# A mixture of experts computed for the chosen experts only, in blocks of 128 rows from two waves of tokens

## The chip, the cores and the metric

The kernel runs on one NeuronCore of a Trainium2 chip. The metric is the device time of one execution in microseconds; three executions of the kernel before took 1513.09, 1513.53 and 1516.65 us (median 1513.53). TensorE is written PE, VectorE DVE, ScalarE ACT, GpSimd POOL, and SyncE, which here only issues DMAs, SP.

## The reference

A block of three residual layers on x of 16 x 64 tokens of 512 values, all in f32:

```python
x = x + xattn(layernorm(x), ctx)        # 16 heads of 64 over pairs of tokens, 512 context tokens
x = x + ssm(layernorm(x))               # projections, conv of 4 taps, selective scan of 16 states, out projection
x = x + moe(layernorm(x))               # below
# moe: T = 1024 tokens, E = 16 experts of I = 256, TOP_K = 4
scores = sigmoid(x @ gate_weight.T); choice = scores + e_bias
# 2 of 4 groups of experts by the sum of the two best, then the 4 best experts in them
topk_weight = scores[topk_idx] / sum
y[t] = sum over e of combine[t, e] * (silu(x @ gate_proj[e].T) * (x @ up_proj[e].T)) @ down_proj[e].T
```

The combine weight of an expert that a token did not choose is 0, so the result is the same whether that expert is computed or not.

## The kernel before, in words

The 1024 tokens are four groups g of 256 (two tiles of 128). Each group goes through attention (8 units of 32 queries x 8 heads, each with its context loaded by SP), projections, and the scan. The scan of group g runs on DVE while PE and ACT do the attention of group g + 1: 16 states, each of four DVE instructions (`scan_step`, L1074, L1077, L1080, L1084) with the decay computed by ACT (L855). The order of every engine is written out by hand in the program of that engine; engines meet at counting semaphores.

After the fourth group's projections comes the expert stage. It computes all 16 experts for all tokens as 64 jobs of one expert and 256 tokens: 48 jobs for groups 0 to 2, expert by expert, then 16 jobs for group 3, whose scan is spread over the first of them (`scan_parts`). A job is `gate_up` (48 matmuls of L634: weights and inputs are split in a rounded and a remainder part, `split_hi` on ACT and `split_lo` on DVE, and three products are summed), tanh on ACT (L902), `hidden` on DVE (L1167, L1168), `down` (four matmuls of 512 columns, L665, each shown as two records) and `add_expert` (L1179), which adds the result times the combine weight to the residual tiles kept in SBUF. Gate, up and down weights of an expert, 512 KB each, are loaded by SP once for groups 0 to 2 and once more for group 3 (`load_raw` L363, `load_down` L376); each of five raw slots is loaded again when DVE has split it. `route` (L1124) computes the combine weights of a group on DVE after its first job. `last_out_proj` (L674) is the out projection of group 3 between jobs. POOL does nothing.

Of the kernel before, what the change touches and what calls it, by code (L numbers as in the profile page):

```python
# [23 lines left out]
F32R = mybir.dt.float32r  # L24
# [32 lines left out]
PIECES = 2  # L57
RAW = 5
CA = G - 1
JA = E * CA  # L60
JOBS = JA + E
SCAN_FROM = 4
SCAN_JOBS = 39
OUT_JOB = SCAN_FROM + SCAN_JOBS + 1
BK_PER_NORM = 512 // (NT * P)
# [19 lines left out]
def job(j):  # L85

    return (j // CA, j // CA, j % CA) if j < JA else (E + j - JA, j - JA, G - 1)


def first_job(c):  # L90
    return c if c < CA else JA


def x_item(j):

    return j + 2 * min(j + 1, CA) + (2 if j >= JA else 0)


def y_item(j):

    return j + (1 if j >= OUT_JOB else 0)


def last_job(k):

    return CA * (k + 1) - 1 if k < E else JA + k - E


def splits(j):


    out = []
    for k in range(1, 2 * E):
        f = CA * k if k < E else JA + k - E
        at = (max(f - 4, -1), f - 3) if k <= E else (f - 2, f - 2)
        out += [(k, p) for p in range(PIECES) if at[p] == j]
    return out


# [4 lines left out]
def scan_parts(j):  # L124

    return [(q // SCAN_PARTS, q % SCAN_PARTS) for q in range(SCAN_PARTS, NS * SCAN_PARTS)
            if SCAN_FROM + (q - SCAN_PARTS) * SCAN_JOBS // ((NS - 1) * SCAN_PARTS) == j]


def perceiver_block(nc, x, ctx_t, ctx_n, wq_t, wk, wv_t, xp_t, dt_t, bc_t, ow_t, gate_t,  # L130
                    eg_t, eu_t, ed_t, params, bc_dram, out):
    with ExitStack() as es:
# [7 lines left out]
        xs_ = sb("x_tokens", G * NT * D)  # L140
# [3 lines left out]
        sb8 = nrm_[0:H, 0:NU * Q].rearrange("p (u h i) -> p u h i", u=NU, h=H)  # L144
        bcT = nrm_[0:2 * NS, 0:GT]
        comb_ = sb("comb", G * NT * E)
        xT_ = sb("normed_t", DC * GT)
        xT = xT_[:, :].rearrange("p (c t) -> p c t", c=DC)
# [6 lines left out]
        acc = acc_[:, :].rearrange("p (k t) -> p k t", k=NBK)  # L155
# [3 lines left out]
        bcs = [bcs_[:, s * 2 * GT:(s + 1) * 2 * GT].rearrange("p (w t) -> p w t", w=2) for s in range(2)]  # L159
# [3 lines left out]
        ident = par[:, C_ID:C_ID + P]  # L163

        lgs = [sb(f"route_logits_{c}", NT * E)[:, :] for c in range(G)]
        sc, sfc, gs = (sb(f"route_{n}", NT * E)[:, :] for n in ("score", "choice", "group"))
        st_ = sb("stats", 6 * G * NT)
        mv_ = sb("mean_var", 2 * NT)
        rstd = sb("rstd", NT)
# [1165 lines left out]
```

## Time and profile before

| what | value |
|---|---|
| median of three runs | 1513.53 us |
| the profiled execution (its span; the page shows no time around it) | 1514.9 us |
| PE busy | 1281.5 us, 85% |
| DVE busy | 1157.1 us, 76% |
| ACT busy | 599.0 us, 40% |
| DMA moved | 128.47 MB, mean 85 GB/s |
| attention, projections, scans of groups 0 to 2 | up to about 858 us |
| expert stage | about 858 us to the end |

A page of the profile gives busy time by engine, the span in 40 slices, the DMA queues, the chain of work that ended last, and groups of instructions. A wait is named by what ended it. Matmuls are pipelined, so the busy time of a PE group overlaps itself; lengths of runs of matmuls in the chain are the better measure. PEclk is TensorE's granted clock as a share of 2.4 GHz; 0.50 is 1.2 GHz.

### The profile page before, as it was taken

What the parts mean: (1) busy time and instruction counts of PE and PEld (TensorE: products, weight loads), DVE (VectorE), ACT (ScalarE), POOL (GpSimd) and SP (SyncE); (2) the same over time, 40 slices, a digit from 0 to 9 for tenths busy, and PEclk for the clock granted to TensorE, in tenths of its full rate; (3) what the DMA queues carried; (4) which work ended last, traced back from release to release, by engine and by line L of the source; (5) the groups of instructions that cost most, each with busy time, mean ns of one, the idle gap of its engine ahead of it and who ended that gap; (6) DMA issues with size and microseconds to landing.
All of it is one profiled execution on the core that took longest, in us unless ns stands there. A gap on an engine that the chain in (4) does not pass through costs nothing.

```text
span 1514.9 us, 16115 instructions
## 1 busy us (share of the span) xinstructions
PE 1281.5 (85%) x6400; PEld 965.9 (64%) x6400; DVE 1157.1 (76%) x1001; ACT 599.0 (40%) x1229; POOL 0.2 (0%) x4
## 2 busy tenths in 40 slices
PE   6998578868859758858758898999999999998998
PEld 4776446646536547536537586777777777676775
DVE  1201899998999998999998848979888888446554
ACT  4432754554655535745536611131313131022220
POOL 0000000000000000000000000000000000000000
PEclk9999878988978978979879789999999999999999
DMA  7333013324013324013314201222222312114553
GB/s 247 101 121 127 6 25 116 104 63 133 8 49 91 118 54 128 10 49 110 89 57 145 91 22 35 86 61 70 56 77 63 84 49 63 56 44 152 168 160 103
DMA packets 95930, 128.47 MB, mean 85 GB/s; under 512 B 4976, under 2 KB 70640, under 8 KB 95856
## 3 DMA queue, kind: packets, MB, share of 16 engines
q1 hardware_dynamic: 95856, 127.45, 27.9%
q8 instruction: 51, 0.84, 0.2%
q14 instruction: 23, 0.19, 0.0%
HBM read 125.21 MB, written 2.23 MB: 84 GB/s over the span
## 4 chain that ended last, share of the span: by engine, by line
DVE 55%; PE 31%; ACT 8%; issue 3%; DMA 2%; DVEq 0%; ACTq 0%; SPq 0%
DVE state L1077 16%; PE bank L634 11%; DVE y_acc L1084 8%; DVE state L1074 8%; DVE state L1080 7%; PE bank L591 6%; PE bank L665 6%; ACT decay L855 4%; DVE x_tokens L1179 3%; DVE w_lo L1161 2%; DMA queries_ctx<-in_dt_t 2%; PE bank L520 2%; PE bank L545 2%; DVE hidden L1168 2%; DVE hidden L1167 2%
## 5 line engine op out<-in xcount | busy, mean ns | idle before, releaser
L1077 DVE TENSOR_TENSOR_SCAN state<-decay,state 128x2048 f32<-128x2048 f32 x64 | 282.9, 4420 | 8.3 <-ACT decay L855 7.2
L665 PE MATMUL bank<-w_down,hidden 128*128 128x512 f32 x512 | 232.1, 596 | 5.2 <-DVE x_tokens L1179 5.2
L634 PE MATMUL bank<-x_hi,w_hi 128*128 128x256 f32 x1024 | 192.6, 312 | 12.2 <-DVE hidden L1168 7.5
L855 ACT ACTIVATE decay<-delta_odd,params 128x256 f32<-128x256 f32 x256 | 106.3, 498 | 197.7 <-DVE state L1077 186.8
L634 PEld LDWEIGHTS bank<-x_hi,w_hi 128*128 128x128 f32 x1024 | 150.3, 198 | 43.5 <-issue 30.4
L520 PE MATMUL bank<-ctx,queries_ctx 128*128 128x256 f32 x512 | 151.8, 449 | 22.2 <-ACT queries_ctx L748 22.2
L634 PE MATMUL bank<-x_hi,w_lo 128*128 128x256 f32 x1024 | 168.9, 288 | 0.0
L634 PE MATMUL bank<-x_lo,w_hi 128*128 128x256 f32 x1024 | 168.7, 288 | 0.0
L902 ACT ACTIVATE hidden<-bank 128x512 f32<-128x512 f32 x64 | 38.0, 594 | 327.6 <-PE bank L665 321.5
L665 PEld LDWEIGHTS bank<-w_down,hidden 128*128 128x128 f32 x512 | 93.3, 191 | 100.5 <-issue 94.2
L1084 DVE TENSOR_TENSOR y_acc<-y_acc,state 128x2048 f32<-128x2048 f32 x64 | 146.7, 2292 | 2.3
L1080 DVE TENSOR_TENSOR state<-state,bc_bcast 128x2048 f32<-128x2048 f32 x64 | 146.2, 2284 | 1.4
L1167 DVE SCALAR_TENSOR_TENSOR hidden<-hidden,bank 128x512 f32<-128x512 f32 x64 | 43.8, 685 | 135.0 <-ACT hidden L902 134.8
L634 PEld LDWEIGHTS bank<-x_hi,w_lo 128*128 128x128 f32 x1024 | 145.6, 198 | 0.0
L634 PEld LDWEIGHTS bank<-x_lo,w_hi 128*128 128x128 f32 x1024 | 145.6, 197 | 0.0
L545 PE MATMUL bank<-probs,ctx 128*128 128x256 f32 x512 | 132.7, 417 | 14.9 <-ACT probs L782 14.9
L520 PEld LDWEIGHTS bank<-ctx,queries_ctx 128*128 128x128 f32 x512 | 109.1, 224 | 53.5 <-ACT queries_ctx L748 23.8
L855 ACT ACTIVATE decay<-delta_even,params 128x256 f32<-128x256 f32 x256 | 107.0, 500 | 79.7 <-DVE state L1077 71.3
L545 PEld LDWEIGHTS bank<-probs,ctx 128*128 128x128 f32 x512 | 104.4, 209 | 40.6 <-ACT probs L782 17.1
L591 PE MATMUL bank<-normed_t,queries_ctx 128*128 128x256 f32 x512 | 112.3, 381 | 2.4 <-DMA queries_ctx<-in_dt_t 1.3
L591 PEld LDWEIGHTS bank<-normed_t,queries_ctx 128*128 128x128 f32 x512 | 96.8, 190 | 19.5 <-DMA queries_ctx<-in_dt_t 3.7
L1161 DVE TENSOR_TENSOR w_lo<-raw_w,w_hi 128x1024 fp32r<-128x1024 f32 x64 | 77.0, 1224 | 33.3 <-ACT w_hi L883 31.9
(128 smaller groups left out, 1328.1 us busy)
## 6 DMA issues: line engine op xcount, KB each, us to landing
ctx<-in_ctx_t SPq DMA_DIRECT2D x32, 512.0 KB, 6.3
ctx<-in_ctx_n SPq DMA_DIRECT2D x32, 512.0 KB, 3.5
bc_bcast<-bc_scratch SPq DMA_DIRECT2D x64, 256.0 KB, 5.1
raw_w<-in_eg_t SPq DMA_DIRECT2D x32, 512.0 KB, 4.3
raw_w<-in_eu_t SPq DMA_DIRECT2D x32, 512.0 KB, 4.0
w_down<-in_ed_t SPq DMA_DIRECT2D x32, 512.0 KB, 4.8
queries_ctx<-in_dt_t SPq DMA_DIRECT2D x4, 2048.0 KB, 10.0
queries_ctx<-in_xp_t SPq DMA_DIRECT2D x4, 2048.0 KB, 14.8
```

Of the source, the lines that this page charges most:

```text
L520: pe.matmul(o, QT[:, k, c, qb * P:(qb + 1) * P], ctxT[n % 2][:, c, :], start=(c == 0), stop=False)
L545: mm = pe.matmul(b[:, cc * Q:(cc + 1) * Q], ctxN[n % 2][:, j, c * P:(c + 1) * P], probT[n % 2][:, j, :], start=(j == 0), stop=(j == KC - 1))
L591: mm = pe.matmul(b[:, kk * GT:(kk + 1) * GT], w[:, c, (k + kk) * P:(k + kk + 1) * P], xT[:, c, :], start=(c == 0), stop=(c == DC - 1))
L634: mm = pe.matmul(o, w[a](k), x[b](k), start=(q == 0), stop=(q == len(terms) - 1))
L665: mm = pe.matmul(b[t][:, :], hid[j % 2][:, i * GT + t * P:i * GT + (t + 1) * P], w_dn[k % 2][:, i, :], start=(i == 0), stop=(i == IC - 1))
L855: ins = act.activation(dA[n % 2][:, k * GT:(k + 1) * GT], dlt[g % 2][:, k, :], ACT.Exp, scale=par[:, c:c + 1])
L1074: step(dve.tensor_tensor(h3, u[g % 2], bs, ALU.mult))
L1077: dve.tensor_tensor_scan(h, dA[n % 2], h, 0.0, ALU.mult, ALU.add).then_inc(scan_rd, 1)
L1080: step(dve.tensor_tensor(h3, h3, cs, ALU.mult))
L1084: dve.tensor_tensor(acc_[:, :], acc_[:, :], h, ALU.add).then_inc(step_done, 1)
L1161: dve.tensor_tensor(lo, raw[q % RAW], hi, ALU.subtract).then_inc(w_rdy, 1)
L1167: step(dve.scalar_tensor_tensor(out=o, in0=o, scalar=1.0, in1=b[0][:, :], op0=ALU.add, op1=ALU.mult))
```

## The change

The expert stage is replaced. Groups 0 and 1 are wave 0, groups 2 and 3 wave 1, of 512 tokens each. For a group, `ffn_norm` (DVE) writes the normed rows, `ffn_logits` (PE, ACT) transposes them and computes logits, `route` (DVE) ranks and masks as before, `positions` (PE, matmuls with 16 columns) counts for each token and expert the earlier tokens of the wave that chose it, and `slots` (DVE) makes from that, for each of a token's four experts, a row of a DRAM tensor: expert e has 512 rows of its own. `dispatch` on POOL scatters each tile's rows there by eight indirect DMAs a group. `block_table` (DVE) turns the counts of a wave into a table in SBUF of 31 entries (expert, first row): as many blocks of 128 rows as 512 x 4 choices can need with 16 experts. All 31 blocks are run, whatever the counts; those beyond the last used one read rows that hold zeros or leftovers and nothing reads their results.

For a block q, SP reads the two entries into registers, loads gate, up and down weights of that expert (three DMAs of 512 KB, 4 KB for each partition, to one of NW = 3 slots) and the 128 rows (256 KB, one of NX = 3 slots), and stores the block's result (256 KB) to DRAM. PE transposes the rows (4), does gate and up as 4 plain f32 matmuls of 512 columns, transposes the hidden values (2) and does down as 2 matmuls of 512 columns. ACT copies the transposes and results out of PSUM. After a wave, `collect` on POOL gathers four rows of each token by indirect DMAs, `combine` (DVE) adds them with their weights, and the tile is stored. The split products, `split_hi`, `split_lo` and `add_expert` are gone.

The norms, logits, routes and slots of groups 0 and 1 are done during the attention of groups 2 and 3; those of group 2 and the scan of group 3 during wave 0; those of group 3, with the out projection of its scan, between the waves. The collecting and combining of wave 0 runs beside wave 1. During the first 14 attention units POOL writes zeros over the scatter tensors: 40 DMAs of up to 512 rows, 41.4 MB in all. The core of the diff:

```diff
--- before.py
+++ after.py
+WAVES = ((0, 1), (2, 3))
+WAVE_OF = [w for g in range(NGR) for w in range(len(WAVES)) if g in WAVES[w]]
+WTILES = [[TILE0[g] + t for g in gs for t in range(NTS[g])] for gs in WAVES]
+CAP = [P * len(t) for t in WTILES]
+BLOCKS = [(TOPK * c + E * (P - 1)) // P for c in CAP]
+BLOCK0 = [sum(BLOCKS[:w]) for w in range(len(WAVES))]
+ROWS = [E * c + b * P - TOPK * c for c, b in zip(CAP, BLOCKS)]
...
+CLEARS = [(w, r, min(r + CLEAR_ROWS, ROWS[w])) for w in range(len(WAVES)) for r in range(0, ROWS[w], CLEAR_ROWS)]
+CLEAR_UNITS = range(1, 15)
...
+NW = 3
+NX = 3
...
+            def load_block_w(w, j):
+                q = BLOCK0[w] + j
+                sp.wait_ge(tab_rdy, w + 1)
+                e = sp.value_load(tabs[w][j:j + 1, 0:1], min_val=0, max_val=E - 1)
+                if q >= NW:
+                    sp.wait_ge(y_full, q - NW + 1)
+                for p, t in enumerate((eg_t, eu_t)):
+                    sp.dma_start(wb_[q % NW][:, p * DC * I:(p + 1) * DC * I],
+                                 t[bass.DynSlice(e, 1)].rearrange("o (p c) i -> p (o c i)", p=P)).then_inc(gu_in[q % NW], 16)
+                sp.dma_start(wb_[q % NW][:, 2 * DC * I:],
+                             ed_t[bass.DynSlice(e, 1)].rearrange("o (p c) d -> p (o c d)", p=P)).then_inc(dn_in[q % NW], 16)
...
+            def load_block_x(w, j):
+                q = BLOCK0[w] + j
+                if j == 0:
+                    sp.wait_ge(tab_rdy, w + 1)
+                    sp.wait_ge(dispatched, 16 * TOPK * sum(len(WTILES[v]) for v in range(w + 1)))
+                row = sp.value_load(tabs[w][j:j + 1, 1:2], min_val=0, max_val=ROWS[w] - P)
+                if q >= NX:
+                    sp.wait_ge(xt_full, q - NX + 1)
+                sp.dma_start(xb[q % NX], xd[w][bass.DynSlice(row, P)]).then_inc(xb_in[q % NX], 16)
+            def store_block_y(w, j):
+                q = BLOCK0[w] + j
+                sp.wait_ge(y_rdy, q + 1)
+                sp.dma_start(yd[w][j * P:(j + 1) * P], yb[q % NX]).then_inc(yb_out[q % NX], 16)
+            def store_out(n, t):
...
+                for j in range(BLOCKS[w]):
+                    if j + NX < BLOCKS[w]:
+                        load_block_x(w, j + NX)
+                    if j + NW < BLOCKS[w]:
+                        load_block_w(w, j + NW)
+                    store_block_y(w, j)
...
-            def split_matmul(o, w, x, chunks):
-                terms = [(a, b, k) for a, b in ((0, 0), (0, 1), (1, 0)) for k in range(chunks)]
-                for q, (a, b, k) in enumerate(terms):
-                    mm = pe.matmul(o, w[a](k), x[b](k), start=(q == 0), stop=(q == len(terms) - 1))
-                return mm
...
-            def gate_up(j):
-                k, e, c = job(j)
-                b = x_pair(x_item(j))
-                if first_job(c) == j:
-                    pe.wait_ge(xm_rdy, c + 1)
-                x_parts = [(lambda q, v=v: v[:, q * GT:(q + 1) * GT]) for v in xm[c % CA]]
-                for p in range(PIECES):
-                    pe.wait_ge(w_rdy, k * PIECES + p + 1)
-                    for i in range(IC):
-                        w_parts = [(lambda q, v=v: v[p][:, q, i * P:(i + 1) * P]) for v in w_gu[k % 2]]
-                        mm = split_matmul(b[p][:, i * GT:(i + 1) * GT], w_parts, x_parts, DC)
-                mm.then_inc(x_full, 1)
...
-            def down(j):
-                k, e, c = job(j)
-                b = y_pair(y_item(j))
-                if j == 0:
-                    pe.wait_ge(d_free, jd.n)
-                    pe.wait_ge(a_free, ja.n)
-                pe.wait_ge(down_in[k % 2], 16 * (k // 2 + 1))
-                pe.wait_ge(h_rdy, j + 1)
-                for t in range(NT):
-                    for i in range(IC):
-                        mm = pe.matmul(b[t][:, :], hid[j % 2][:, i * GT + t * P:i * GT + (t + 1) * P],
-                                       w_dn[k % 2][:, i, :], start=(i == 0), stop=(i == IC - 1))
+            def block_x_t(q):
...
+            def block_x_t(q):
+                pe.wait_ge(xb_in[q % NX], 16 * (q // NX + 1))
+                if q >= 2:
+                    pe.wait_ge(xt_rdy, q - 1)
+                v = xb[q % NX].rearrange("t (p c) -> t c p", c=DC)
+                for c in range(DC):
+                    mm = pe.transpose(bank[q % 2][:, c * P:(c + 1) * P], v[:, c, :], ident)
+                mm.then_inc(xt_full, 1)
+            def gate_up(q):
+                pe.wait_ge(xt_rdy, q + 1)
+                pe.wait_ge(gu_in[q % NW], 32 * (q // NW + 1))
+                if q >= 2:
+                    pe.wait_ge(h_rdy, q - 1)
+                o = bank[2 + q % 2][:, :].rearrange("p (g i) -> p g i", g=2)
+                for c in range(DC):
+                    mm = pe.matmul(o, xbT[q % 2][:, c, :], w_gu[q % NW][:, :, c, :], start=(c == 0), stop=(c == DC - 1))
+                mm.then_inc(gu_full, 1)
+            def hidden_t(q):
+                pe.wait_ge(h_rdy, q + 1)
+                b = job_a()
+                v = hid[q % 2].rearrange("t (p c) -> t c p", c=IC)
+                for c in range(IC):
+                    mm = pe.transpose(b[:, c * P:(c + 1) * P], v[:, c, :], ident)
+                mm.then_inc(a_full, 1)
+                ha[q] = ja.n
+            def down(q):
+                pe.wait_ge(a_free, ha.pop(q))
+                pe.wait_ge(dn_in[q % NW], 16 * (q // NW + 1))
+                if q >= 2:
+                    pe.wait_ge(y_rdy, q - 1)
+                for c in range(IC):
+                    mm = pe.matmul(bank[4 + q % 2][:, :], hidT[q % 2][:, c, :], w_dn[q % NW][:, c, :],
+                                   start=(c == 0), stop=(c == IC - 1))
                 mm.then_inc(y_full, 1)
-            def last_out_proj():
-                b = y_pair(y_item(OUT_JOB) - 1)
-                pe.wait_ge(step_done, NS * G)
...
+            def experts(w):
+                q0, n = BLOCK0[w], BLOCKS[w]
+                pe.wait_ge(d_free, jd.n)
+                for j in range(-2, n + 1):
+                    if j + 2 < n:
+                        block_x_t(q0 + j + 2)
+                    if 0 <= j + 1 < n:
+                        gate_up(q0 + j + 1)
+                    if 0 <= j - 1:
+                        down(q0 + j - 1)
+                    if 0 <= j < n:
+                        hidden_t(q0 + j)
+                    if w == 0 and j == 0:
+                        ffn_logits(NGR - 2)
+                    if w == 0 and j == 4:
+                        positions(NGR - 2)
             pe.wait_ge(par_in, 16)
             pe.wait_ge(ones_rdy, 1)
-            norm_transposes(0, NT)
+            norm_transposes(0, NTS[0])
             attention(0)
...
+            experts(0)
+            pe.wait_ge(y_rdy, BLOCK0[1])
+            out_proj(NGR - 1)
+            ffn_logits(NGR - 1)
+            positions(NGR - 1)
+            experts(1)
...
+            def keep_y(q):
+                act.wait_ge(y_full, q + 1)
+                if q >= NX:
+                    act.wait_ge(yb_out[q % NX], 16 * (q // NX))
+                act.activation(yb[q % NX], bank[4 + q % 2][:, :], ACT.Copy).then_inc(y_rdy, 1)
...
-            def split_lo(k, p):
-                q = k * PIECES + p
-                dve.wait_ge(w_hi_rdy, q + 1)
-                hi, lo = (v[p].rearrange("p c i -> p (c i)") for v in w_gu[k % 2])
-                dve.tensor_tensor(lo, raw[q % RAW], hi, ALU.subtract).then_inc(w_rdy, 1)
...
+            def hidden(q):
+                b = bank[2 + q % 2]
+                dve.wait_ge(th_rdy, q + 1)
+                o = hid[q % 2]
+                step(dve.scalar_tensor_tensor(out=o, in0=o, scalar=1.0, in1=b[:, 0:I], op0=ALU.add, op1=ALU.mult))
+                dve.tensor_tensor(o, o, b[:, I:2 * I], ALU.mult).then_inc(h_rdy, 1)
...
+                if w == 0:
+                    add_tiles(NGR - 1)
+                    ffn_norm(NGR - 1)
+                    route(NGR - 1)
+                    slots(NGR - 1)
+                    block_table(1)
+                    out_slots(1)
+            for i, t in enumerate(WTILES[1]):
+                combine(len(WTILES[0]) + i, t)
...
+                pool.wait_ge(s_full, n)
+                v = xd[w][first:end].rearrange("(p r) d -> p r d", p=P)
+                pool.dma_start(v, fx_[:, 0:D].unsqueeze(1).to_broadcast([P, (end - first) // P, D])).then_inc(cleared, 16)
...
+            def dispatch(c):
+                pool.wait_ge(slot_rdy, c + 1)
+                for t in range(NTS[c]):
+                    for k in range(TOPK):
+                        i = (TILE0[c] + t) * TOPK + k
+                        pool.indirect_dma_start(xd[WAVE_OF[c]], bass.IndirectOffsetOnAxis(slot[:, i:i + 1].bitcast(U32), 0),
+                                                fx[:, t, :], None).then_inc(dispatched, 16)
...
+                    pool.indirect_dma_start(yg_[n % 2][:, k, :], None, yd[w],
+                                            bass.IndirectOffsetOnAxis(yslot[:, i:i + 1].bitcast(U32), 0))\
+                        .then_inc(yg_in[n % 2], 16)
...
```

## Rows read from the trace of the kernel before

**Rows 1.** The page of the profile: the span, and busy time of each engine.
```profile
span 1514.9 us, 16115 instructions
...
PE 1281.5 (85%) x6400; PEld 965.9 (64%) x6400; DVE 1157.1 (76%) x1001; ACT 599.0 (40%) x1229; POOL 0.2 (0%) x4
```

**Rows 2.** Windows (length, busy by engine, PEclk, DMA share, GB/s): attention, experts.
```profile
617.00:779.00 162.00, 120.17 (x496) 85.00 (x496) 158.59 (x73) 89.69 (x222) 0.00 (x0) 0.86 0.24 63
858.00:1514.90 656.90, 623.72 (x3632) 488.56 (x3632) 464.37 (x534) 152.52 (x258) 0.00 (x0) 0.97 0.28 83
```

**Rows 3.** Chain that ended last: start us, us, what.
```profile
1251.12 5.75 PE bank L634 x48
1256.87 3.44 PE bank L665 x8
...
1311.98 13.73 PE bank L674 x32
```

**Rows 4.** Groups of instructions by line and form: busy us, mean ns, idle before.
```profile
L1077 DVE TENSOR_TENSOR_SCAN state<-decay,state 128x2048 f32<-128x2048 f32 x64 | 282.9, 4420 | 8.3 <-ACT decay L855 7.2
L665 PE MATMUL bank<-w_down,hidden 128*128 128x512 f32 x512 | 232.1, 596 | 5.2 <-DVE x_tokens L1179 5.2
...
L1084 DVE TENSOR_TENSOR y_acc<-y_acc,state 128x2048 f32<-128x2048 f32 x64 | 146.7, 2292 | 2.3
...
L1161 DVE TENSOR_TENSOR w_lo<-raw_w,w_hi 128x1024 fp32r<-128x1024 f32 x64 | 77.0, 1224 | 33.3 <-ACT w_hi L883 31.9
...
L902 ACT ACTIVATE hidden<-bank 128x512 f32<-128x512 f32 x64 | 38.0, 594 | 327.6 <-PE bank L665 321.5 <-PE bank L634 6.1
...
L1095 DVE TENSOR_TENSOR rank_scratch<-route_choice 128x256 f32<-128x256 f32 x8 | 3.4, 421 | 0.1
```

**Rows 5.** Timeline of PE (start us, us): eight 128x128 transposes.
```profile
826.17 1.04 PE L620 MATMUL bank<-params,normed 128*128 128x128 f32 x8
```

**Rows 6.** Timeline of SP's queue, 787 to 790 us: start us, issue us.
```profile
788.24 0.37 SPq L348 DMA_DIRECT2D queries_ctx<-in_dt_t  x1
788.66 0.51 SPq L349 DMA_DIRECT2D queries_ctx<-in_xp_t  x1
```

**Rows 7.** Windows: large loads in flight, the clock around idle PE.
```profile
788.00:792.00 4.00, 0.37 (x2) 0.37 (x3) 3.35 (x9) 0.30 (x1) 0.00 (x0) 0.50 0.48 81
791.60:797.70 6.10, 5.00 (x16) 2.81 (x16) 5.55 (x9) 1.27 (x3) 0.00 (x0) 0.50 0.96 388
797.70:802.00 4.30, 4.00 (x19) 3.25 (x18) 4.27 (x2) 0.37 (x1) 0.00 (x0) 1.00 1.03 408
856.70:859.20 2.50, 0.01 (x1) 0.00 (x0) 2.43 (x4) 2.47 (x6) 0.00 (x0) 0.98 0.23 73
863.50:872.80 9.30, 9.21 (x43) 9.24 (x44) 5.40 (x11) 3.96 (x5) 0.00 (x0) 0.50 0.61 187
381.30:384.70 3.40, 1.17 (x9) 0.84 (x8) 2.29 (x6) 3.38 (x5) 0.00 (x0) 0.99 0.01 2
384.70:388.10 3.40, 3.40 (x8) 1.85 (x7) 3.33 (x7) 1.92 (x2) 0.00 (x0) 0.51 0.00 0
```

**Rows 8.** DMA issues of the page: KB each, median us from issue to landing.
```profile
ctx<-in_ctx_n SPq DMA_DIRECT2D x32, 512.0 KB, 3.5
...
raw_w<-in_eg_t SPq DMA_DIRECT2D x32, 512.0 KB, 4.3
```

**Rows 9.** Timeline of DVE: first and last of 33 instructions of one route.
```profile
895.21 0.18 DVE L1128 TENSOR_SCALAR route_score<-route_logits 128x32 f32<-128x32 f32 x1
...
903.57 0.19 DVE L1155 TENSOR_TENSOR comb<-route_score,route_group 128x32 f32<-128x32 f32 x1
```

**Rows 10.** Timelines, 787 to 832 us: norm of one group on DVE, an ACT table load.
```profile
788.30 1.42 DVE L989 BATCH_NORM_STATS2 stats<-x_tokens 128x6 f32<-128x512 f32 x2
...
790.57 1.00 DVE L1001 TENSOR_SCALAR normed<-x_tokens,mean_var,rstd 128x512 f32<-128x512 f32 x2
...
830.91 1.28 ACT L724 ACT_TABLE_LOAD   x1
```

More of the change, by code:

```diff
@@ new lines, in attention_units @@
+                    if k == 1 and g >= 2:
+                        positions(g - 2)
+                    if now:
+                        scan_decay(g - 1, now[0], NBK // 2)
+                    copy_probs(n)
+                    for s in now[1:]:
+                        scan_decay(g - 1, s)
+                keep_ctx(g, NUS[g] - 1)
+            def projections(g):
+                late = list(range(NS - TAIL + 1, NS)) if g > 0 else []
+                norm_std(NTS[g])
+                norm_copy(xT[g], NTS[g])
@@ L995, in norm_stats, with norm_apply @@
                 step(dve.reciprocal(std[:, first:first + n], std[:, first:first + n]))
-            def norm_apply(tile0, slot, var=mv_, std=rstd, first=0):
-                for t in range(NT):
+            def norm_apply(tile0, n, slot, var=mv_, std=rstd, first=0):
+                for t in range(n):
                     q = first + t
@@ L1120, in free_logits @@
[L1120 to L1133 removed]
+                step(dve.tensor_reduce(out, rk1.rearrange("p (r j) -> p r j", j=n), AX_X, ALU.add))
@@ new lines, in hidden, with combine @@
+            def hidden(q):
[4 more added lines that the diff above has]
+                dve.tensor_tensor(o, o, b[:, I:2 * I], ALU.mult).then_inc(h_rdy, 1)
+            def combine(n, t):
+                dve.wait_ge(yg_in[n % 2], 16 * TOPK * (n // 2 + 1))
+                tile = xs[:, t, :]
+                for k in range(TOPK):
+                    c = t * TOPK + k
+                    ins = dve.scalar_tensor_tensor(out=tile, in0=yg_[n % 2][:, k, :], scalar=wk[:, c:c + 1], in1=tile,
+                                                   op0=ALU.mult, op1=ALU.add)
+                    if k < TOPK - 1:
+                        step(ins)
+                ins.then_inc(comb_done, 1)
@@ L1219, in _ @@
             scan_inputs(0)
-            scan_step(0, 0, parts=(0, 1, 2))
-            scan_step(0, 0, parts=(3,))
-            for g in range(G - 1):
+            dve.wait_ge(cst_rdy, 1)
+            step(dve.tensor_copy(iota[:, :], iota_i[:, :]))
+            scan_step(0, 0)
+            for g in range(NGR - 1):
                 for s in range(LEAD):
@@ L1285, in _ @@
-            add_expert(JOBS - 1)
-            dve.nop().then_inc(out_rdy, 1)
+            for w in range(len(WAVES)):
+                q0, n = BLOCK0[w], BLOCKS[w]
+                for j in range(-1, n):
+                    if j + 1 < n:
+                        hidden(q0 + j + 1)
+                    if w == 0:
+                        if j == 1:
+                            route(NGR - 2)
+                        if j == 5:
+                            slots(NGR - 2)
+                        for state, part in scan_parts(j):
+                            scan_step(NGR - 1, state, parts=(part,))
+                    elif j >= 2 and j % 2 == 0 and (j - 2) // 2 in range(len(WTILES[0])):
+                        combine((j - 2) // 2, WTILES[0][(j - 2) // 2])
+                if w == 0:
+                    add_tiles(NGR - 1)
[4 more added lines that the diff above has]
+                    out_slots(1)
```

1015 lines of the change are left out of this document (554 added, 461 removed).

## The prediction

> **What bounds the kernel now.** The page comes first [rows 1]: PE is busy for 85% of 1514.9 us and DVE for 76%, neither bound everywhere, so the span has to be cut into stages. The windows [rows 2] do that. While a group's attention runs beside the scan of the group before, DVE is busy for 158.6 of 162 us: whatever is added to DVE there lengthens the span by itself. From 858 us on it is PE, 623.7 of 656.9 us at a clock of 0.97. The chain of waits [rows 3] gives the step of that stage: 48 matmuls of gate and up in 5.75 us, four of down in 3.44 us, so 9.19 us a job and 588 us for 64 jobs; 13.7 us of out projection and the norms and logits make up the rest. Down's 3.44 us for four also gives the price of a plain f32 matmul of 512 columns at full clock, 0.86 us.
>
> **PE's work after.** A block has four transposes (eight take 1.04 us [rows 5], so 0.52), four matmuls for gate and up (3.44), two transposes (0.26) and two for down (1.72): 5.9 us. Two waves of 31 blocks make 184 us each, 368 against 588. DVE has, in wave 0, 15 scan states of 4.42 + 3 x 2.29 = 11.3 us [rows 4], 31 times two instructions of 256 columns at 0.42 (26 us), a route of 8.5 us (33 instructions from 895.21 to 903.76 [rows 9]) and about 3 us of slots: 208 us, 6.7 a block. Were these the bounds, the change would win. They aren't, by the order in which the loads are released.
>
> **The new wait: a block's loads hang on the block before.** The weights of block j+3 go into the slot of block j and are issued when down of j has ended (y_full). PE's order is rows of j+4, gate and up of j+3, down of j+1: between down of j and gate and up of j+3 stand only six transposes, 0.8 us. Down of j+1, which releases the next load, comes behind that gate and up. So from one y_full to the next PE first waits for a load, then works 0.52 + 3.44 + 1.72 = 5.7 us, and nothing of this overlaps. The rows are worse placed than the weights. On SP's queue each turn is: rows of j+3, weights of j+3 (held for y_full of j), store of block j. The rows of j+4 are therefore issued behind the weights of j+3 and the store, and they are what PE transposes ahead of gate and up of j+3.
>
> **L, from y_full to the landing of those rows.** Issues take 0.37 to 0.51 us each [rows 6]: three for weights, one store, one for rows, about 2.4 us, and between the last two a read of a register from the table, which no row shows. Its ends are 0 and the 3.5 us of a small load's round trip [rows 8]; I take 1, near the low end, as a few bytes need no large transfer. The rows are then issued at 3.4 us. They share the DMA engines with the rest: the first large load at 788.24 meets a window to 792 with a DMA share of 0.48, that is 1.92 us busy, so data flow 1.84 us after an issue, and then at 388 to 408 GB/s with the engines 96 to 103% busy [rows 7]. A turn moves 3 x 524 KB + 2 x 262 KB = 2.10 MB, 5.1 us at 408. With 0.3 us to complete, L = 1.84 + 5.1 + 0.3 = 7.3 us. Ends: gate and up alone (1.05 MB) 4.4 us, and 9.4 us where the register read costs 3.5 and the rows then land in 3.5. The Trainium skill (DMA: Bandwidth & Descriptors, Specifications) gives a core's HBM limit as about 358 GB/s; the windows show 408, so the measurement decides, and by the page L would be 7.7 and the total some 20 us more.
>
> **The clock.** PE idles about 7 us in each turn. In the trace the clock is at 0.50 from 2.5 us after PE stopped at 856.7, and stays there for 9.3 us after it resumed at 863.5; after the idle before 791.6 for 6.1; after the short idle before 384.7 for 3.4 [rows 7]. I take 4.75, between the shorter two, since matmuls here are dense: they do 2.4 of the 5.7 us of work, the other 3.3 run at full clock, 8.1 in all. Turn: 7.3 + 8.1 = 15.4, say 15.5 us. Ends: 4.4 + 5.7 = 10.1 (never cold, early landing) and 9.4 + 11.4 = 20.8 (all cold).
>
> **The sum**, against the profiled span, which is 1.4 us (0.1%) over the median of the runs.
> - Attention, DVE-bound: two routes 17, two times slots 6, a block table and output slots 5 (some 20 instructions of 0.2 to 0.4 us), three norms of 3.3 us (788.30 to 791.57) and an ACT table load of 1.28 with its wait [rows 10], 15. Out: a norm 3.3, two w_lo of 1.2, four instructions of 512 columns at 0.6 [rows 4], 8. Net 35.
> - The 41.4 MB of zeros run on POOL's queue beside context loads. Some 23 MB fall in the eight units of group 0, whose PE is not covered by a scan; at 408 GB/s they take 56 us, and a context load may be late by a few: 5, between 0 and 56. The rest hides behind DVE. First rows of wave 0, issue and landing: 5. Logits of group 2 inside wave 0: 5. PE thus has 858 + 35 + 5 + 5 + 5 = 908 before the waves count.
> - Waves: 3 blocks each are loaded ahead, 7 us each; 28 at 15.5: 455 each, 910.
> - Between the waves nothing overlaps: copy 0.6, out projection 13.7, add 0.7, norm and table load 4.6, transposes and copies 2.2, logits 3, table load and exp 1.5, route 8.5, positions and copy 3.4, slots 3, eight scatters and their landing 15.5, first rows 4, PE cold at times 1.3: 62.
> - After the last block: copy and store 4.1, sixteen gathers in four tiles with only two buffers, combine 2.5 a tile, store 3.5: 36. No row shows an indirect DMA. Its ends are an ordinary issue, 0.37, and one that lands before the next, 4.3 [rows 6, 8]; I take 1.5, nearer to the issue, because only issue has to be serial. The ends move both terms together by -27 and +62.
>
> 908 + 910 + 62 + 36 = 1916; I say **1915 us**.
>
> **Rivals.** *Early landing or a warm clock (1690 us, 0.17).* If the weights' landing alone counts, or the clock holds, the turn is 10 to 13 us; at 11.5 the sum is 56 x 4 = 224 less. For it: the queue may let the small rows through. Against: the engines are 96% busy while large loads are in flight [rows 7].
> *Colder and later (2165 us, 0.15).* The register read and the address taken from a register cost several us and every block is cold: turn 20, 56 x 4.5 = 252 more. For it: PE idles 7 us in each turn, and 9.3 us cold have been seen; nothing of before reads a register.
> *The loads are hidden and the change wins (1412 us, 0.04).* The mechanism is the prefetch: if L is over before PE arrives, wave 0 goes at DVE's 7.0 and wave 1 at PE's 6.1: 908 + 217 + 189 + 62 + 36. Break-even with 1515 needs a turn of (1515 - 908 - 62 - 36 - 42) / 56 = 8.3 us, that is L of 2.6 us or less at a full clock. A single load of 512 KB takes 3.5 to 4.3 [rows 8], and three of them, a store and the rows are asked for here.
> *The change doesn't do what it says (0.01).* Were unused blocks skipped, fewer turns would run; but the loops over 31 have no branch.
>
> **Numbers.** The forecast has 0.63. Its own range: a turn of 12.6 (4.4 + 8.1) takes 162 off and quick POOL issues 27, about 1725; cold for 9.3 us (work 4.65 in it, 1.05 after: 10.4, turn 17.7) adds 123 and slow POOL issues 35, about 2075. From 1720 to 2080 it also takes in a part of the first two rivals, 8 in 10. A measurement of this kernel tells 0.3% (about 4.5 us) from no change. Faster only with the hidden loads or skipped blocks: 0.05; within 0.3%: 0.01; slower: 0.94.
>
> **What would show it.** Weight loads waiting for down on SP; PE's rows transposes waiting for the DMA of the rows, about 7 us in each of 56 turns; y_full every 15.5 us in both waves alike, though only wave 0 has the scan; a granted clock near 0.65 in the waves; DMA near 135 GB/s (2.10 MB a turn); DVE done early in wave 0; PE without blocks for some 60 us between the waves. Wrong would be: y_full every 6 to 8 us, a wave 0 clearly longer than wave 1 (then DVE's scan sets it), or a wait for the weights but none for the rows.

## The result, and the profile after the change

The changed kernel takes 2033.14 us (median of 4 runs, 2026.34 to 2036.74), the kernel before beside it 1513.97 (1513.09 to 1516.65): a ratio of 1.342, interval 1.338 to 1.345. The forecast was slower, 1915 us, range 1720 to 2080. The direction, the mechanism and the range held; 118 us are missing from the sum.

The page of the profile after: span, busy time, the chain's shares, and DMA issues (KB each, us from issue to landing). The first lines answer to [rows 1], the last ones to [rows 8].

```profile
span 2035.0 us, 12399 instructions
...
PE 1193.0 (59%) x3988; PEld 747.9 (37%) x3988; DVE 990.2 (49%) x934; ACT 617.9 (30%) x1350; POOL 119.5 (6%) x113
...
PE 35%; DVE 27%; DMA 22%; SPq 6%; issue 5%; ACT 4%; POOL 0%; POOLq 0%; DVEq 0%; ACTq 0%
DMA block_x<-dispatched 16%; PE bank L723 15%; DVE state L1218 8%; PE bank L742 5%; PE bank L691 5%; DVE y_acc L1225 4%; DVE state L1221 4%; DVE state L1215 4%; DMA ctx<-in_ctx_t 4%; PE bank L713 3%; PE bank L618 2%; SPq L409 2%; DMA queries_ctx<-in_dt_t 2%; PE bank L641 2%; SPq L420 1%
...
ctx<-in_ctx_t SPq DMA_DIRECT2D x32, 512.0 KB, 7.6
...
block_x<-dispatched SPq DMA_DIRECT2D x62, 256.0 KB, 6.1
```

PE has 88 us less to do than before and DVE 167 less, and yet the span is 520 us longer. In the expert stage no engine is busy throughout any more; DVE's 27% of the chain is the attention and scans of before. What has come in is a line of the chain that did not exist, the landing of a block's rows, with 16% of the chain.

The windows by stage (columns as in [rows 2]: length, busy time and instructions by engine, PEclk, DMA share, GB/s): wave 0, what lies between the waves, wave 1, and what follows the last block.

```profile
926.00:1439.00 513.00, 249.06 (x573) 124.79 (x571) 199.64 (x166) 102.52 (x237) 12.73 (x8) 0.70 0.39 127
1439.00:1507.00 68.00, 23.92 (x78) 15.36 (x78) 20.98 (x79) 5.24 (x9) 15.32 (x16) 0.66 0.38 146
1507.00:2002.00 495.00, 250.18 (x558) 123.31 (x558) 37.78 (x78) 56.84 (x123) 7.56 (x8) 0.71 0.37 126
2002.00:2035.00 33.00, 0.15 (x1) 0.00 (x0) 12.03 (x16) 0.60 (x1) 16.01 (x16) 0.57 0.55 167
```

The two waves are nearly equally long, though DVE has 200 us of work in the one and 38 in the other: DVE does not set them. PE is busy for half of each at a clock of 0.70, DMA for 0.38. So neither engine nor bandwidth fills the stage: it goes by a chain in which each waits for the other.

One turn of wave 1 in the timeline, PE first (start us, us, idle before and releaser), then SP's queue:

```profile
1708.48 1.88 PE L742 MATMUL bank<-expert_w,hidden_t 128*128 128x512 f32 x4
1710.20 0.39 PE L732 MATMUL bank<-params,hidden 128*128 128x128 f32 x2
1719.00 1.13 PE L713 MATMUL bank<-params,block_x 128*128 128x128 f32 x4 [8.41 <-DMA block_x<-dispatched]
1719.92 5.27 PE L723 MATMUL bank<-expert_w,block_x_t 128*128 128x512 f32 x8
1725.03 1.88 PE L742 MATMUL bank<-expert_w,hidden_t 128*128 128x512 f32 x4
```

```profile
1710.54 0.35 SPq L409 DMA_DIRECT2D expert_w<-in_eg_t  x1
...
1711.89 0.42 SPq L428 DMA_DIRECT2D expert_out<-block_y  x1
1713.07 0.34 SPq L423 DMA_DIRECT2D block_x<-dispatched  x1
```

Down of one block ends at 1710.36 (1708.48 + 1.88) and releases, 0.18 us later, five issues (up and down at 1710.98 and 1711.45, not shown), the rows last. They land at 1719.00, 8.64 us behind down, and only then PE works: 7.9 us to the end of the next down. Over a wave a turn is 17.3 us in wave 0 and 17.0 in wave 1 (27 turns each, 950.2 to 1418.3 and 1521.8 to 1980.8). The waits of the whole kernel (us in total, times, longest), and PE's last wait of wave 0:

```profile
PE bank L713 <- DMA block_x<-dispatched: 497.9, 56, 11.9
...
SPq L409 <- PE bank L742: 728.9, 56, 26.2
```

```profile
1425.70 5.67 PE L723 MATMUL bank<-expert_w,block_x_t 128*128 128x512 f32 x8 [5.26 <-issue]
```

SP's queue waits for down 56 times, 28 in each of two waves, as counted. The equal count of PE's waits for rows is a coincidence: two of the 56 (11.91 and 0.23 us) come ahead of wave 0's first blocks. In the turns there are 27 such waits a wave, 54 in all with 485.8 us, since the rows of blocks 4 to 30 are the late ones. The 28th turn of each wave has no rows left to wait for and stands only for the last block's gate and up weights: it takes 12.9 and 13.6 us. The wait for rows is thus 9.0 us on average, and with the 0.23 us in which PE still transposes hidden, L is 9.2 us.

### The profile page after: what moved, and what is told of

It reads as the page before. It is cut to its first block, busy times and chain, and to the rows that moved or that the text cites. A ratio compares the mean times of both kernels' runs of the same rounds, so it can differ in the third digit from the quotient of the medians.

```text
span 2035.0 us, 12399 instructions
## 1 busy us (share of the span) xinstructions
PE 1193.0 (59%) x3988; PEld 747.9 (37%) x3988; DVE 990.2 (49%) x934; ACT 617.9 (30%) x1350; POOL 119.5 (6%) x113
## 4 chain that ended last, share of the span: by engine, by line
PE 35%; DVE 27%; DMA 22%; SPq 6%; issue 5%; ACT 4%; POOL 0%; POOLq 0%; DVEq 0%; ACTq 0%
DMA block_x<-dispatched 16%; PE bank L723 15%; DVE state L1218 8%; PE bank L742 5%; PE bank L691 5%; DVE y_acc L1225 4%; DVE state L1221 4%; DVE state L1215 4%; DMA ctx<-in_ctx_t 4%; PE bank L713 3%; PE bank L618 2%; SPq L409 2%; DMA queries_ctx<-in_dt_t 2%; PE bank L641 2%; SPq L420 1%
## 5 line engine op out<-in xcount | busy, mean ns | idle before, releaser
L1362 DVE SCALAR_TENSOR_TENSOR hidden<-hidden,bank 128x256 f32<-128x256 f32 x62 | 26.1, 421 | 785.3 <-ACT hidden L1027 785.3
L713 PE MATMUL bank<-params,block_x 128*128 128x128 f32 x248 | 68.1, 428 | 526.6 <-DMA block_x<-dispatched 497.9
L723 PE MATMUL bank<-expert_w,block_x_t 128*128 128x512 f32 x496 | 324.0, 813 | 11.2 <-issue 11.2
L1218 DVE TENSOR_TENSOR_SCAN state<-decay,state 128x2048 f32<-128x2048 f32 x64 | 282.9, 4420 | 14.4 <-ACT decay L973 13.6
L713 PEld LDWEIGHTS bank<-params,block_x 128*128 128x128 f32 x248 | 45.1, 218 | 539.0 <-DMA block_x<-dispatched 496.5
L723 PEld LDWEIGHTS bank<-expert_w,block_x_t 128*128 128x128 f32 x496 | 132.0, 281 | 164.7 <-issue 164.3
L1023 ACT ACTIVATE block_x_t<-bank 128x512 f32<-128x512 f32 x62 | 37.0, 596 | 447.2 <-PE bank L713 447.1
L641 PE MATMUL bank<-probs,ctx 128*128 128x256 f32 x512 | 131.0, 413 | 17.8 <-ACT probs L897 13.8
L1501 POOL DMA_INDIRECT dispatched<-ffn_x,slot x32 | 58.0, 1812 | 1118.7 <-DVE slot L1307 1110.2
L641 PEld LDWEIGHTS bank<-probs,ctx 128*128 128x128 f32 x512 | 103.2, 207 | 43.3 <-ACT probs L897 15.9
L742 PE MATMUL bank<-expert_w,hidden_t 128*128 128x512 f32 x248 | 117.0, 594 | 2.9 <-ACT hidden_t L1037 2.9
L1027 ACT ACTIVATE hidden<-bank 128x256 f32<-128x256 f32 x62 | 23.8, 383 | 277.9 <-PE bank L723 277.9
L1215 DVE TENSOR_TENSOR state<-u_even,bc_bcast 128x2048 f32<-128x2048 f32 x32 | 73.4, 2292 | 4.1 <-DMA bc_bcast<-bc_scratch 2.7
L1215 DVE TENSOR_TENSOR state<-u_odd,bc_bcast 128x2048 f32<-128x2048 f32 x32 | 73.3, 2291 | 1.0
```

The costliest lines, as they stand in the source:

```text
L641: mm = pe.matmul(b[:, cc * Q:(cc + 1) * Q], ctxN[n % 2][:, j, c * P:(c + 1) * P], probT[n % 2][:, j, :], start=(j == 0), stop=(j == KC - 1))
L713: mm = pe.transpose(bank[q % 2][:, c * P:(c + 1) * P], v[:, c, :], ident)
L723: mm = pe.matmul(o, xbT[q % 2][:, c, :], w_gu[q % NW][:, :, c, :], start=(c == 0), stop=(c == DC - 1))
L742: mm = pe.matmul(bank[4 + q % 2][:, :], hidT[q % 2][:, c, :], w_dn[q % NW][:, c, :], start=(c == 0), stop=(c == IC - 1))
L1215: step(dve.tensor_tensor(h3, u[g], bs, ALU.mult))
L1218: dve.tensor_tensor_scan(h, dA[n % 2][:, 0:sw], h, 0.0, ALU.mult, ALU.add).then_inc(scan_rd, 1)
```

## The experiments

All are variants of the changed kernel; the kernel before ran beside each (1514.99 us beside the first four, 1516.19 and 1515.78 beside the others). In their order below they are called rows4, w4, rows4_w4, tiny_w, warm8, late_zeros, rows6_w4_zeros and rows6_w4_spread. rows4, w4 and tiny_w ran once each, warm8 twice, the others four or five times. Diffs are cut to their core.

### A fourth slot for rows

```diff
+NR = 4
...
-        xb = [sb(f"block_x_{s}", D)[:, :] for s in range(NX)]
+        xb = [sb(f"block_x_{s}", D)[:, :] for s in range(NR)]
...
-                    if j + NX < BLOCKS[w]:
-                        load_block_x(w, j + NX)
+                    if j + NR < BLOCKS[w]:
+                        load_block_x(w, j + NR)
```

NX stays 3 for the results, block_y.

> Four slots for a block's rows in place of three, so that rows of block j+4 are issued ahead of the weights of block j+3 and a whole turn before PE wants them. Theory A (each turn waits for loads that are released by the down of two blocks before, and the rows land last, 8.5 us after it): the rows leave the path, gate and up weights stay on it with some 5.5 us, and the transposes run inside that wait. Turn 17.1 - 3.0 - 0.9 = 13.2, clock permitting, so about 2035 - 56 x 3.9 = 1817 us. Rival B (the DMA engines or SP cannot deliver 2.1 MB and its issues faster, whatever the order): turn unchanged, about 2035.

Measured: 1843.35 us, 190 less than the changed kernel and 26 more than expected. The timeline of PE in one turn with ACT's copy of the transposed rows, and PE's largest wait:

```profile
1706.19 1.88 PE L743 MATMUL bank<-expert_w,hidden_t 128*128 128x512 f32 x4
...
1708.13 0.65 PE L714 MATMUL bank<-params,block_x 128*128 128x128 f32 x4
...
1708.86 0.60 ACT L1024 ACTIVATE block_x_t<-bank 128x512 f32<-128x512 f32 x1
...
1713.72 6.27 PE L724 MATMUL bank<-expert_w,block_x_t 128*128 128x512 f32 x8 [4.95 <-issue]
```

```profile
PE bank L724 <- issue: 271.1, 55, 5.4
```

The rows are there already (their transposes follow down at once) and PE stands at gate and up instead, 5.65 us behind down (1708.07 to 1713.72). The trace names no releaser for it; by the program gate and up wait for the copied rows (there at 1709.46), for the hidden values of two blocks before (long done) and for their weights, whose first issue was at 1708.24, behind that down. So it is the weights. A turn is 13.6 us in both waves, 3.5 less. The terms: PE stands for 5.65 us behind down where it stood for 9.2 (the rows' extra lateness, 3.5), the transposes now run inside the wait (0.9), and gate and up takes 6.27 us instead of 5.27, which gives 1.0 back and was not in the expectation. Behind the wait for rows stands the second wait that the prediction names, the weights' own.

### A fourth slot for weights

```diff
-NW = 3
+NW = 4
+NPRE = 3
...
             sp.wait_ge(ys_rdy, NGR)
+            for j in range(NPRE, NW):
+                load_block_w(0, j)
```

Ahead of wave 0 three blocks' weights are loaded in the attention, as before, and the fourth behind it.

> Four slots for weights, three for rows, so weights come one turn earlier but the rows are still issued behind weights and store of the block before. Theory A: nothing is gained, as the rows are what lands last: 2035 +- 15 us. A rival by which the weights set the turn: turn falls to 8 or less, total near 1530 us.

Measured: 2022.92 us in its one run, 10 under the median of the changed kernel and 3 under its fastest. The wait for the rows stands where it was, and wave 1 still takes 17.0 us a turn:

```profile
PE bank L716 <- DMA block_x<-dispatched: 500.9, 55, 16.1
```

The weights are now a block ahead, and wave 1's turns gain nothing from it, since SP's queue is in order: the rows are issued behind the weights and the store that wait for down, whatever slot the weights go to.

### Both

The two diffs together.

> Four slots for both. Theory A: no load hangs on the block before any more; wave 0 goes at DVE's 6.8 us a block, wave 1 at PE's 6.0 to 6.4, so the waves take about 420 instead of 1015 us: about 1450 us, ratio to before 0.96. Rival B (bandwidth or issue binds): turn 12 or more, at least 1780 us. With part of the engines' time lost to contention, turns of 8 give about 1520.

Measured: 1568.43 us, ratio 1.034 (1.030 to 1.038): 465 us less than the changed kernel, but 118 more than expected. Two turns of PE in wave 1:

```profile
1303.24 1.88 PE L746 MATMUL bank<-expert_w,hidden_t 128*128 128x512 f32 x4
...
1305.67 3.60 PE L727 MATMUL bank<-expert_w,block_x_t 128*128 128x512 f32 x8
1309.11 1.88 PE L746 MATMUL bank<-expert_w,hidden_t 128*128 128x512 f32 x4
...
1313.67 1.13 PE L717 MATMUL bank<-params,block_x 128*128 128x128 f32 x4 [2.46 <-DMA block_x<-dispatched]
1314.60 4.66 PE L727 MATMUL bank<-expert_w,block_x_t 128*128 128x512 f32 x8
```

One turn is 5.87 us (1303.24 to 1309.11), PE's own work as the prediction summed it (5.9). The next waits again for rows, and behind the idle time gate and up takes 4.66 instead of 3.60. 29 waits for rows make 116.6 us, 16.9 of them the one ahead of wave 0. What the expectation missed: one more slot moves the rows one turn ahead, and a turn that has shrunk to 5.9 us is shorter than their way (issued 2.5 us behind down, landing 6 later).

### Hardly any weights

A block's loads after the first three take 128 of the 1024 columns of each third; the number and order of issues stay.

```diff
+                n = DC * I if j < NW else 128
-                    sp.dma_start(wb_[q % NW][:, p * DC * I:(p + 1) * DC * I], ...)
+                    sp.dma_start(wb_[q % NW][:, p * DC * I:p * DC * I + n], ...[:, 0:n])
```

> The weights of a block after the first three are loaded only to 128 of 1024 columns of each third (512 B for a partition in place of 4 KB), so most of the weights are left out; order, waits and number of DMAs are those of the changed kernel. If the 1.57 MB ahead of the rows delay them (theory A), the rows land at about 2.6 + 3.0 = 5.6 instead of 8.5 us after down, turn about 13.9, total about 1855 us. If it is the chain of issues and the latency of a load by itself (rival C), the turn stays within 1 us of 17.1, total over 1980.

Measured: 1882.76 us. The page's issue line of the rows, and PE's wait in one turn of wave 1:

```profile
block_x<-dispatched SPq DMA_DIRECT2D x62, 256.0 KB, 2.6
```

```profile
1706.79 1.88 PE L743 MATMUL bank<-expert_w,hidden_t 128*128 128x512 f32 x4
...
1713.95 1.13 PE L714 MATMUL bank<-params,block_x 128*128 128x128 f32 x4 [5.06 <-DMA block_x<-dispatched]
```

The rows land 2.6 us after their issue instead of 6.1, so 3.5 us of their way is the weights' data ahead of them; L is 5.3 (1708.67 to 1713.95) and the turn 13.6 in wave 1, as expected. In wave 0 it is 15.3, which was not. SP's queue there:

```profile
1181.14 0.42 SPq L429 DMA_DIRECT2D expert_out<-block_y  x1
1181.62 0.42 SPq L398 DMA_DIRECT2D bc_bcast<-bc_scratch  x1
1183.23 0.35 SPq L424 DMA_DIRECT2D block_x<-dispatched  x1
```

In most second turns the scan's 256 KB broadcast of B and C stands between the store and the rows; the rows of this one reached PE at 1187.72, 7.9 us after PE stopped. The turns mostly alternate, 16.8 and 13.8. The 28 us over the expectation are these.

### TensorE kept busy in the wait

```diff
-                pe.wait_ge(xb_in[q % NX], 16 * (q // NX + 1))
                 if q >= 2:
                     pe.wait_ge(xt_rdy, q - 1)
+                for _ in range(8 if q % BLOCKS[0] >= NX else 0):
+                    pe.matmul(bank[q % 2][:, :], ident, ow[:, 0, :], start=True, stop=True)
+                pe.wait_ge(xb_in[q % NX], 16 * (q // NX + 1))
```

> Turn theory (a turn of a wave is L, the way from the last down matmul over weights and rows to the landed rows, plus the work behind it, and a cold TensorE only stretches that work): eight matmuls that nobody reads (128 columns of the identity by 512 columns of out_w) stand ahead of TensorE's wait for the rows, so that it is busy in most of the 8.5 us of L. L stays at 8.5 us. If TensorE is then granted its higher clock, gate/up falls from 5.3 to about 3.5 us and the rest by about 0.5, the turn goes from 17.1 to about 15, and over 56 turns some 110 us go: 2033 to about 1920, granted clock from 0.77 to 0.85 or more. Rival: the clock does not matter or the dummies take as long as L themselves (8 x 0.87 us cold is 7 us): 2033 within 20 us or above it.

Measured: 1958.76 us, ratio 1.291 (1.287 to 1.295) against 1.342. The timeline of one turn:

```profile
1771.21 7.03 PE L711 MATMUL bank<-out_w,params 128*128 128x512 f32 x16
1779.42 0.75 PE L715 MATMUL bank<-params,block_x 128*128 128x128 f32 x4 [1.17 <-DMA block_x<-dispatched]
1780.00 3.60 PE L725 MATMUL bank<-expert_w,block_x_t 128*128 128x512 f32 x8
1783.44 1.88 PE L744 MATMUL bank<-expert_w,hidden_t 128*128 128x512 f32 x4
```

L is 8.3 us (1771.15 to 1779.42) and the work behind it 5.9. Granted clock in wave 1: 0.99 (1545 to 1900 us), where it was 0.70. Turns of 14.2 us are the rule there, 14.8 the mean, 15.9 in wave 0. Adding work to the busiest path shortens the kernel by 74 us: that is what the higher clock gives back, less what the dummies cost. The rival's price for them was misread: eight in 7 us is the higher level, as here; at the lower one each of the two records of such a matmul takes 0.85 us (gate and up of rows4, 1714.71 to 1718.12), so eight would take some 13.6 us, an estimate, and outlast L. The gain fell short of the expected 110 by the dummies ahead of the fourth block of each wave, whose rows come without such a wait, so that they stand there for 7 us in full (the first down is at 957.4 for 950.2, and from the last down of wave 0 to the first of wave 1 it is 91.7 us for 84.8), and by wave 0's broadcasts.

### The zeros later

```diff
-CLEAR_UNITS = range(1, 15)
+CLEAR_UNITS = (8,) * 8 + (9, 10, 11, 12, 13, 14)
```

> Theory: the zeros written to memory in the units of group 0 (23 of the 40 writes, 1 MB each in three descriptors' worth of POOL issue) slow the context loads there, and that cost group 0's attention 24 us (dt_t asked for at 146.06 instead of 122.24). Moved to units 8 to 14, where VectorE sets the pace and the queues are at less than half their rate, they should cost nothing: dt_t of group 0 back at 122 to 125, the total at 2009 to 2014 (2033 less 20 to 24). Rival: the cost moves with the zeros, since the context loads there are needed as soon: 2025 or more, and dt_t of the later groups later by what the first gains.

Measured: 2027.61 us, ratio 1.336 (1.333 to 1.339) against 1.342 (1.338 to 1.345), a gain of about 6 us at the edge of what can be told. The periods between the loads of dt_t, a projection's weights asked for when a group's attention ends, show why. Before (groups 0 to 2), the changed kernel (0 to 2), and this one (0 and 1, then the stretch in which its zeros go out):

```profile
0.00:122.24 122.24, 104.39 (x504) 77.91 (x504) 18.73 (x46) 51.11 (x107) 0.20 (x4) 1.00 0.43 146
122.24:343.52 221.28, 157.25 (x648) 116.30 (x648) 188.20 (x112) 115.66 (x258) 0.00 (x0) 0.84 0.26 75
343.52:565.82 222.30, 169.12 (x680) 119.89 (x680) 212.07 (x122) 118.86 (x266) 0.00 (x0) 0.85 0.26 76
```

```profile
0.00:146.06 146.06, 113.75 (x504) 82.80 (x504) 19.77 (x48) 51.14 (x107) 17.91 (x32) 0.93 0.77 285
146.06:370.62 224.56, 154.89 (x648) 114.09 (x648) 188.44 (x115) 115.98 (x258) 12.39 (x17) 0.83 0.45 153
370.62:610.51 239.89, 171.46 (x710) 123.96 (x710) 224.47 (x176) 123.15 (x273) 22.03 (x8) 0.84 0.26 79
```

```profile
0.00:127.68 127.68, 106.60 (x504) 79.52 (x504) 19.77 (x48) 51.14 (x107) 18.16 (x32) 0.97 0.61 216
127.68:362.20 234.52, 159.76 (x648) 117.40 (x648) 188.43 (x115) 115.87 (x258) 12.43 (x17) 0.78 0.58 206
...
110.00:150.00 40.00, 26.84 (x121) 19.12 (x122) 5.12 (x13) 6.24 (x11) 4.55 (x7) 0.69 1.02 401
```

Group 0 gains 18.4 us and group 1 gives 10 back. Its DVE work is the same (188.43 us); the first scan step comes 60.2 us behind the load of dt_t (187.8), 51.6 before (197.7 behind 146.06), because dt_t and x_proj, which the scan needs, are loaded while 23 zero writes fill the queues (share 1.02). The zeros' cost moved with them, as the rival said, though not in full.

### Six slots for rows, four for weights, the zeros later

> Six row slots, four weight slots and the late zeros. Theory: with four and four a turn is TensorE's own 5.9 us except where the rows, issued 2.5 us behind a down matmul and landing 6 us later, come late: 117 us in 29 waits, and the cold matmuls behind each. With six slots the rows are asked for two turns sooner, so those waits go, and the zeros give back 22: 1568 - 22 - about 90 = 1440 to 1480, which is faster than before (ratio about 0.96). Rival: DMA is the bound by then (1.5 MB of weights and 0.5 MB of rows in 5.9 us are 357 GB/s, where 408 was the most seen): the waits turn into waits for the weights, gate/up waits instead of the transposes, and the total stays at 1530 to 1560.

Measured: 1491.45 us, ratio 0.984 (0.981 to 0.986): 1.6% below the kernel before, and 11 us above the expected band. Turns are 8.2 us in wave 0 and 6.2 in wave 1. A stretch of wave 1 in the windows, the largest of PE's waits in wave 0 (900 to 1180 us), and ACT at one of them:

```profile
1280.00:1420.00 140.00, 133.49 (x405) 68.10 (x405) 29.68 (x60) 39.67 (x91) 7.57 (x8) 1.00 1.00 360
```

```profile
PE bank L727 <- ACT block_x_t L1027: 45.0, 12, 12.2
```

```profile
1154.30 3.30 ACT L977 ACTIVATE decay<-delta_odd,params 128x256 f32<-128x256 f32 x8 [4.67 <-DVE state L1222]
1157.51 0.57 ACT L1027 ACTIVATE block_x_t<-bank 128x512 f32<-128x512 f32 x1
```

In wave 1 the waits for rows are gone; PE is busy for 95% at its higher level and the DMA engines for all of the time at 360 GB/s, so PE and DMA are both at their bound: 2.10 MB a turn at 360 are 5.8 us, PE's work is 5.9. In wave 0 the copy of the transposed rows stands in ACT's queue behind a decay that waits for the scan on DVE, 45 us in 12 waits. No run changes ACT's order, so this rests on the trace alone. It is DVE reaching PE through ACT's order, where the prediction had expected DVE's sum alone (6.7 to 7.0 us a block).

### The zeros one unit later still

```diff
-CLEAR_UNITS = (8,) * 8 + (9, 10, 11, 12, 13, 14)
+CLEAR_UNITS = range(9, 15)
```

> As rows6_w4_zeros, but the zeros start one unit of keys later (units 9 to 14 in place of 8 to 14, seven writes behind each), so that none stands in the queues when dt_t and x_proj of group 0 are loaded. Theory: in late_zeros 23 writes went out together at 97.2 us, the queues were full from 110 to 150 us (share 1.02, 401 GB/s), and of the 18.4 us that group 0's attention gained, the wait for u_even gave 8.5 back. With the new place the first scan step starts at about 178 us instead of 187.8, the total is 1478 to 1485. Rival: the zeros are in the way of the keys of group 1 instead (their writes and 208 to 342 GB/s of loads fall together between 230 and 310 us), and the total stays within 3 us of 1491 or is above it.

Measured: 1489.14 us, ratio 0.981 (0.979 to 0.983); not told apart from the version before it, so the rival held. The first scan step did start sooner, at 172.8 us (178 was expected) where it was at 185.5 in the version before it and at 187.8 with the late zeros alone. Group 0's attention, with no zero written before its end, and the stretch in which DVE is then idle for more than a quarter:

```profile
0.00:121.60 121.60, 104.24 (x504) 77.80 (x504) 19.77 (x48) 51.12 (x107) 0.84 (x9) 1.00 0.43 146
...
270.00:310.00 40.00, 26.54 (x92) 19.15 (x90) 28.47 (x16) 17.57 (x45) 1.19 (x2) 0.73 1.01 398
```

The first line is the kernel before's again, clock, DMA share and rate included: the 24 us that the changed kernel loses there are the zeros'. In the version before this one DVE was busy for 35.0 us of that second stretch. dt_t of group 1 is asked for at 356.45, of group 3 at 843.92 (rows6_w4_zeros: 361.20, 844.92). Three places for 41 MB of zeros have each cost something; leaving them out wasn't tried, because the rows that no token fills would then be read without having been written.

## Why the prediction was right, and by how much its terms were off

The sizes, from the profiled span: forecast 908 + 910 + 62 + 36 = 1916; measured 918.6 + 520.4 + 68 + 495 + 33 = 2035.

- **The new wait: right.** The turn is L plus the work behind it, on rows first and weights behind them. Taking the rows' lateness away gave 3.5 us a turn, the weights' slot alone nothing, both together brought PE's own 5.9 us in one turn of two. The 28 turns a wave, the equal waves (within 0.3 us a turn) and the DMA rate (forecast 135 GB/s, seen 126 to 127) are as foretold; the clock is 0.70, 0.65 was forecast. The count was one too high for the rows: they are waited for in 27 turns a wave, and the last one, on weights alone, is 2 to 3 us shorter than the 15.5 that the sum takes for it.
- **L: mis-sized, and this is most of the miss.** 9.2 us on average, 7.3 forecast; 1.9 in each of 54 turns are 103 us. The turn as a whole is 17.2 against the 15.5 taken, as the work behind L is 0.1 shorter and 15.4 had been rounded up: that makes 90 of the 119 us, less 4.5 in the two last turns. The other terms: 11 ahead of wave 0, some 20 at the head and tail of the waves (the wait of 7.9 for group 2's logits is one, and 5 for it stood in the 908), 6 between them, -3 at the end. The part of L that was mis-sized is the rate. The issues were nearly right: the rows went out 2.7 us behind down (3.4 forecast) and the gap that holds the register read is 0.76 us (1 taken). Data flow from about 1711.6 us, 1.1 behind the first issue, where 1.84 was taken; so the start was even a little early. But they flow more slowly. The changed kernel in the turn above, the last line being the middle of the flow:

```profile
1709.00:1712.00 3.00, 1.59 (x6) 0.68 (x4) 0.84 (x2) 0.94 (x3) 0.00 (x0) 1.00 0.12 38
1712.00:1719.00 7.00, 0.00 (x0) 0.00 (x0) 0.00 (x0) 0.00 (x0) 0.00 (x0) 0.57 0.81 283
1713.00:1718.00 5.00, 0.00 (x0) 0.00 (x0) 0.00 (x0) 0.00 (x0) 0.00 (x0) 0.50 0.88 302
```

  2.09 MB (38 x 3.0 and 283 x 7.0) took 7.4 us to the start of PE, where 5.1 and another 0.3 to complete, for which there was no row, were forecast from the 408 GB/s of a stretch full of queued loads [rows 7]. Not only the beginning and the end are thin: in the middle too the share is 0.88 and the rate 302 GB/s. Why, no run shows. Even with the engines busy throughout, wave 1 of rows6_w4_zeros shows 360. The Trainium skill (DMA: Bandwidth & Descriptors, Specifications) has about 358 GB/s as a core's limit, which the prediction set aside for the 408: 358 is within 1% of that full wave, but the 401 of late_zeros' stretch of zeros is again above it, so no run here shows it to be a limit. The prediction's own sum by that figure is off: 2.10 MB at 358 are 5.9 us, so L would be 8.0 and the total some 40 us more, where it says 7.7 and 20.
- **The work behind L: right.** 7.9 us in the turn shown against 8.1. warm8 gives its warm value, 5.9 (5.7 forecast), so the cold clock costs some 2.0 us of work a turn.
- **The zeros: mis-sized.** 5 us forecast between 0 and 56; group 0 took 23.8 longer (146.06 against 122.24), and with no zeros in it 121.6. The page has the context loads landing after 7.6 us where it had 6.3 before, PE waited for them for 11 us, and the mean clock of the period is 0.93 for 1.00. How much of the 24 reaches the end is less clear: moving the zeros gained 6 us in all, and the kernel without them wasn't run.
- **DVE's additions: about right, 35 forecast.** Group 1's period grew by 3.3 us, group 2's by 17.6, group 3's by 20.8: 41.7. Of group 2's, 12.4 are DVE work (224.47 against 212.07) and the rest waits. With the zeros it is 65.5 at the dt_t of group 3; 60.6 are left where PE takes the first rows, at 918.6 for the 858 of before (it waits 11.9 for them, 5 forecast), and 50 were forecast, 5 of them for logits that in fact stand inside wave 0 (a wait of 7.9 us there).
- **Between the waves 68 for 62, after the last block 33 for 36.** No row had shown an indirect DMA; nearly all gathers and 18 of the 32 scatters, all eight of those between the waves among them, issue in 0.95 us with 0.30 between, 1.25, where 1.5 was taken between 0.37 and 4.3. (Twenty-four of them at 4.3 would have added 67 us, where the prediction has 62.)
- **Rivals.** "Early landing" needed a turn of 10 to 13, "colder and later" one of 20; both are excluded by 17.0 to 17.3. The total itself lies nearly as close to the second's 2165 (132 us) as to the forecast (118), but not by that rival's cause: the register read and the address cost 0.76 us, and gate and up, 5.27 us in the changed kernel and 6.27 in rows4, is not all cold. "Loads hidden" gave 1412 as the price if the prefetch reached: with six and four slots the profiled span is 1488, and 48 of the 76 us between lie in wave 0, where ACT's order adds its waits; 14 lie between the waves, 8 ahead of them and 7 in wave 1, where DMA comes to its bound. "Does not do what it says" is excluded: 62 blocks ran, and SP waited for the slot of 56 of them.

## What to carry to other kernels

A ring of k slots hides a load only if the slot's release stands far enough ahead of the use in the *consumer's own order*: write down, for each ring, the event that frees the slot, everything that the issuing queue has ahead of the load, and the engine's work between that event and the use. Do it for the smallest load too; here 256 KB of rows, last in an in-order queue behind 1.5 MB of weights, landed 3.5 us behind the weights and so set the turn. When work falls by a third but comes in 62 short steps that depend on each other, first count the slots, and expect a second wait behind the first (here 4.9 us behind one of 9.0). For a burst that drains to its last byte take the rate of a burst (here 283 GB/s), not that of full queues (408).

## What the runs showed of the hardware that was not expected

- Eight dummy matmuls in each wait (7.03 us) made the kernel 74 us faster (warm8): granted clock of wave 1 from 0.70 to 0.99, gate and up from 5.27 to 3.60 us.
- With the DMA engines fully busy the rate was 401 GB/s with zeros and context loads (late_zeros, 110 to 150 us) and 360 with weights, rows, stores and gathers (rows6_w4_zeros, 1280 to 1420): the share alone doesn't tell the rate.
- Reading a register from the table and computing the address held SP for 0.76 us between two issues (1711.89 + 0.42 to 1713.07).
- A plain write of zeros, 1 MB, holds POOL for 0.75 us (17.32 us for 23 of them in late_zeros), and an indirect scatter of 128 rows for 0.96 (18 of 32) to 4.69.
